# Layer 1's pair loop of a two-layer graph kernel: exponential and lower half moved one pair behind, product three pairs behind

## The reference, cut to what matters

```python
XW = X @ W
Z1 = leaky_relu(s_row[:, None] + s_col[None, :], negative_slope=0.01)   # s_col = XW @ a[:f], s_row = XW @ a[f:]
den = exp(Z1)                                  # 2708 x 2708
num = A @ den
att = where(num != 0, den / num, 0)
H = A @ (att @ XW)
x = layernorm(x + H)
```

## Time and profile before

| | |
|---|---|
| median of 3 runs | 820.3 us (819.61 to 824.0) |
| the profiled execution | 821.94 us, its span 820.2 us |
| layer 1's pair loop, first "ln" to last "ln" | 448.37 to 726.00 us of the span |
| PE, DVE, ACT, POOL busy over the span | 79%, 77%, 52%, 48% |
| mean granted TensorE clock | 0.919 of full |

### The profile page before, as it was taken

The page is one execution under the profiler, slowest core; times in us unless marked ns, Lnnn a source line. Parts: engine busy times, 40 slices in busy tenths (PEclk is TensorE's granted clock), DMA queues, the critical chain, the costliest instruction groups (busy, mean ns, idle before and its releaser), DMA issues.

```text
span 820.2 us, 12721 instructions
## 1 busy us (share of the span) xinstructions
PE 649.0 (79%) x4284; PEld 364.8 (44%) x4284; DVE 634.1 (77%) x1278; ACT 425.0 (52%) x611; POOL 394.1 (48%) x449
## 2 busy tenths in 40 slices
PE   5589999999979898745977678778878778764894
PEld 5244333433329687633532233333333333223783
DVE  3599999999987589988775477787878878782462
ACT  2388888888861156884533254554554555440000
POOL 6378888777770567734717886000000000006685
PEclk9999999999977899955995699999999999995998
DMA  9953444980000000024941000000000000014110
GB/s 210 208 98 68 70 86 84 391 354 1 1 4 1 14 22 14 14 85 136 410 202 46 24 1 1 2 1 1 1 1 2 1 1 2 1 50 134 36 39 24
DMA packets 24554, 58.30 MB, mean 71 GB/s; under 512 B 2634, under 2 KB 13918, under 8 KB 24478
## 3 DMA queue, kind: packets, MB, share of 16 engines
q0 software_dynamic: 7744, 33.39, 16.1%
q1 hardware_dynamic: 16734, 23.92, 8.1%
HBM read 51.59 MB, written 20.96 MB: 88 GB/s over the span
## 4 chain that ended last, share of the span: by engine, by line
DVE 37%; issue 17%; PE 16%; POOL 12%; ACT 12%; DMA 3%; DVEq 2%; POOLq 0%; ACTq 0%; SPq 0%
DVE R L795 7%; DVE ring L786 6%; DVE ring L1198 6%; ACT ring L662 5%; POOL X L439 3%; PE PSALL L1353 3%; DVE ring L1179 2%; PE PSALL L1333 2%; POOL X L462 2%; POOL ring L474 2%; DVE AO L1198 2%; ACT AO L662 2%; PE PSALL L1281 2%; POOL AT L433 2%; DVE R L1108 2%
## 5 line engine op out<-in xcount | busy, mean ns | idle before, releaser
L382 POOL TENSOR_TENSOR R<-R,ring 128x452 f32<-128x452 f32 (+1 forms) x126 | 152.7, 1215 | 33.2 <-ACT ring L503 31.6
L795 DVE SCALAR_TENSOR_TENSOR R<-ring,R 128x452 bf16<-128x452 f32 (+1 forms) x132 | 134.9, 1023 | 0.2
L1541 PE MATMUL PSALL<-AT,R 128*128 x432 | 94.5, 362 | 41.5 <-ACT R L658 39.7
L1333 PE MATMUL PSALL<-R,AO 128*128 128x452 bf16 (+2 forms) x396 | 100.6, 364 | 17.1 <-DVE R L795 16.0
L458 POOL MEMSET R<- 128x108 f32 x1 | 0.2, 188 | 224.0 <-PE PSALL L1577 224.0
L503 ACT ACTIVATE ring<-ring,sm 128x452 f32<-128x452 f32 (+1 forms) x132 | 88.3, 669 | 29.7 <-DVE ring L786 23.5
L1281 PE MATMUL PSALL<-XN 128*128 128x452 f16 (+2 forms) x396 | 98.8, 360 | 4.7 <-issue 4.2
L1353 PE MATMUL PSALL<-R,AT 128*128 128x256 f16 (+1 forms) x792 | 94.1, 279 | 0.0
L1185 DVE TENSOR_TENSOR ring<-ring 128x904 bf16<-128x904 f32 (+1 forms) x50 | 60.6, 1212 | 42.8 <-ACT ring L662 42.8
L511 ACT ACTIVATE R<-ring,sm 128x452 bf16<-128x452 f32 (+1 forms) x132 | 88.6, 671 | 4.3
L662 ACT ACTIVATE ring<-ring 128x904 f32<-128x904 f32 (+1 forms) x50 | 47.8, 956 | 71.3 <-DVE ring L1198 71.3
(11 more groups left out here) (260 smaller groups left out, 1105.2 us busy)
## 6 DMA issues: line engine op xcount, KB each, us to landing
AT<-in_adjT POOLq DMA_DIRECT2D x22, 677.0 KB, 7.1
ATd<-AT SPq DMA_DIRECT2D x2, 7447.0 KB, 31.0
XWd<-ring SPq DMA_DIRECT2D x11, 128.0 KB, 1.8
x1d<-AO SPq DMA_DIRECT2D x1, 1408.0 KB, 6.0
out<-ring SPq DMA_DIRECT2D x21, 64.0 KB, 1.5
Yd<-R SPq DMA_DIRECT2D x1, 768.0 KB, 3.7
Yd<-R SPq DMA_DIRECT2D x1, 640.0 KB, 4.3
AT<-ATd,idx POOLq DMA_INDIRECT x22, 8.5
```

Of the source, the lines that this page charges most:

```text
L382: i = G.tensor_tensor(ES_, ES_, z, ALU.add)
L795: V.scalar_tensor_tensor(F[0:rows, RW:RW + w], z, 1.0, F[0:rows, 0:w], ALU.subtract, ALU.subtract).then_inc(s_low, 1)
L1333: m = TE.matmul(PSALL[:, c, 0:w], half_[0:rows, jt, :], F[0:rows, o:o + w], start=(jt == 0 and k == 0), stop=(jt == T - 1 and k == 2))
L1541: TE.matmul(PSALL[:, b, 0:w], den_h[:, s + q, :, part], AT[:, q:T, c0:c0 + w][:, bass.ds(first, 1), :].rearrange("p o j -> p (o j)"), star ...
```

## The change

`LAG` goes from 2 to 3. On ACT "exp" of pair v-1 follows "ln" of pair v, and "den exp" moves from the turn with cp 0 to that with cp 1, behind that "exp". On DVE "sub" comes first in a pair's turn, then low of v-1, scores of v+1, den scores where cp is 0; "den halves" moves from the turn with cp 1 to the end of the turn with cp 2. A last "exp" follows ACT's loop. No instruction is added, removed or resized.

```diff
-        LAG = 2
+        LAG = 3
@@ scalar
+            def attention_exp(v):
+                av.wait_ge(s_sub, v + 1)
+                S.activation(z_of(v), z_of(v), ACT.Exp).then_inc(s_att1, 1)
+
             for v in range(NV):
...
                 S.activation(tL.rearrange("p (q w) -> p q w", q=2), PSALL[:, 6:8, 0:RW], ACT.Ln, bias=tiny).then_inc(s_ln, 1)
-                if cp == 0 and jt + 1 < T:
+                if v:
+                    attention_exp(v - 1)
+                if cp == 1 and jt + 1 < T:
                     den_exp(jt + 1, 0)
-                av.wait_ge(s_sub, v + 1)
-                S.activation(z_of(v), z_of(v), ACT.Exp).then_inc(s_att1, 1)
                 if cp == 2 and jt + 1 < T:
                     den_exp(jt + 1, 1)
                 if v == 6:
                     S.activation(erb, rb[:, 0:N], ACT.Exp, scale=SLOPE / (1.0 - SLOPE)).then_inc(s_erb, 1)
+            attention_exp(NV - 1)
@@ vector
             for v in range(NV):
                 jt, cp = v // 3, v % 3
+                dv.wait_ge(s_ln, v + 1)
+                dv.wait_ge(s_z1, v + 1)
+                V.tensor_tensor(z_of(v), z_of(v), tL[:, 0:wide_of(v)[1]], ALU.subtract).then_inc(s_sub, 1)
                 if v:
                     attention_low(v - 1)
                 if v + 1 < NV:
                     attention_scores(v + 1)
                 if cp == 0 and jt + 1 < T:
                     den_scores(jt + 1)
-                dv.wait_ge(s_ln, v + 1)
-                dv.wait_ge(s_z1, v + 1)
-                V.tensor_tensor(z_of(v), z_of(v), tL[:, 0:wide_of(v)[1]], ALU.subtract).then_inc(s_sub, 1)
-                if cp == 1 and jt + 1 < T:
+                if cp == 2 and jt + 1 < T:
                     den_halves(jt + 1)
-                if cp == 2 and jt + 1 < T:
                     den_all(jt + 1)
             attention_low(NV - 1)
```

## The result

The changed kernel took 865.9 us (865.3 to 867.3, 4 runs) against 820.2 us (819.6 to 824.0): a ratio of 1.055 (95% interval 1.052 to 1.058), 46 us slower. The forecast was 877, its range 857 to 889. The profiled execution of after took 866.6 us, its span 864.7 us, with a mean granted clock of 0.893 (before 0.919).

What follows compares the result with a forecast made beforehand. Bound by the chain sub, exp, low, scores. Regular tiles +36.5 us, tiles 3, 7, 8, 9 and 19 +17.0, tiles 0 to 2 +2.9, tiles 20 and 21 0: +56 on 821.9, 877 us on the median's basis; range 857 to 889.

Steps and rivals of the forecast that it cites:

- The cycle of the banks: PE with its two banks: 1.30 us from ln to num plus 2.12 us to the next ln, 3.42 us a pair.
- Exp one pair behind: On ACT: exp of the pair before costs nothing and takes 0.96 us off DVE's chain, with 0.1 us to spare.
- The wait on den halves: At each change of tile num starts 4.62 us after ln, not 1.30; a full-clock tile takes 13.58 us against 12.21.
- the opposite case: Rival, kernel gets faster: first num of a tile not held by den halves, under 1.4 us of wait left; chance 0.05.
- The clock: At each change of tile PE idles 3.46 us, its clock falls and the next num takes 1.67 us more.
- the 12 regular tiles: Tiles 4 to 6 and 10 to 18: 15.25 us each against 12.21, together +36.5 us.
- The row that I leaned on: Trace before, behind the long exponential: after a 3.79 us PE gap the clock fell; num took 3.79 us instead of 2.12.
- The upper bound of 2.5 us: Clock loss at a change of tile if the slower clock lasts through the product: 6 matmuls of 2.42 us, not 1.36.
- Product three pairs behind: Scores of v+1 waits for a product ended 2 us earlier: free, except 0.1 us at the end of the loop.
- The start of the loop: Tiles 0 to 2: num of pair 3 ahead of the product, 2.8 us sooner; tiles 1 and 2 slower; together +2.9 us.
- With the clock kept: Rival: the clock stays up through PE's 3.46 us gaps at changes of tile, 33 us less, about 843 us; chance 0.12.
- With den halves in time: Rival: den halves doesn't hold a tile's first num, 10.26 us a tile against 12.21, 787 us; chance 0.05.

Runs made afterwards that it cites:

- The first experiment: The changed kernel with den halves back at the end of the turn with cp 1, one pair earlier: 779.9 us, ratio 0.948.
- the filler kernel: The changed kernel with 12 matmuls more per tile but the first, ahead of num's wait on den halves, results overwritten: 841.7 us, ratio 1.024.
- LAG 2 with early loads: The changed kernel with den halves back at cp 1, LAG 2 again and PE's register loads for the next tile ahead of the product: ratio 0.961.

## Why the prediction was right, and where its size was off

- **The limits.** The cycle of the banks, worked out as 3.42 us, was 3.41 and 3.42 us for a regular "num" at full clock in every kernel in which exp is a pair behind.
- **Exp one pair behind.** Right: low never waits for it, the 0.1 us of room was enough. It is exp alone that moved: low of pair v-1 stood in pair v's turn before the change too, and the lower half that the title has one pair later is den halves. The first experiment shows the gain of exp and the lag together, 42 us.
- **The wait on den halves.** Right in place, count and size: num 4.54 us after ln (forecast 4.62), a tile of 13.5 us at full clock (13.58), and shown as cause by the first experiment and by two more places of the same call. Only the bound for the opposite case was too strict: faster was to need less than 1.4 us of the wait, but with 1.6 us left (2.91 - 1.30, den halves right behind sub) the kernel was already 10 us faster. By the sum's own terms the point is 1.95 us.
- **The clock.** Right in mechanism, mis-sized. The term was 1.67 us at every change of tile. A lost one costs 1.6 to 1.9 us, and 0.4 to 0.5 more where it lasts into the next pair, but only 11 of 18 were lost. Over the 12 regular tiles the forecast was 36.5 us and the measured sum 12 x (14.48 - 12.21) = 27 us: this is nearly the whole difference between the forecast of +57 and the +46 measured. Of these 9 us the clock is 8 (1.67 - 0.98 = 0.69 us a tile, with 14.48 - 13.5 = 0.98 measured), the distances one. The row that I leaned on, one gap of 3.79 us, could not say that a gap of the same length may end either way. Nor was 1.78 us the nearest gap at full clock in that trace: behind the loop PE was idle for 2.46 us up to 766.58 and the granted clock stayed at 1.00, and ahead of the loop a gap of 3.44 us up to 431.43 lost it. The upper bound of 2.5 us comes to 1.67 + 1.06 = 2.73 us by the rows it names; nothing else rests on it. By the Trainium skill's page "TensorE: Matmul & The Clock Gate", section "Loop structure matters more than you think", the loop nest decides whether matmuls stay at speed, and a long wait (for a DMA, in its example) in front of each runs them cold. The filler kernel agrees: with the wait filled, the clock of 520 to 760 us is 1.00 and not 0.91. But 7 of the 18 unfilled waits kept the clock, and there the measurement decides.
- **Product three pairs behind.** "Free" was right for this kernel, as scores comes late in DVE's new turn. It was not for the reason given alone: I looked at the data and the buffers, not at what else is queued behind a wait. In the old order the same LAG costs about 2%, and in the new order LAG 2 costs 0.9 us a tile.
- **The start of the loop.** Its +2.9 us came out as +2.8, in part by luck. The ln of pair 3 was to come 4.62 + 3.35 = 7.97 us after that of pair 2 and came 8.89 us after it, while the two distances before it were 0.95 us shorter than I had left them (9.18 against 10.13). The 3.35 us stand in no row; that num took 3.99 us.
- **The rivals.** With the clock kept I gave 843; the filler kernel took 841.7. With den halves in time I gave 787; the first experiment took 779.9. The second was too high because I had taken little of the gain at the loop's start: the first three tiles took 39.0 us there and 47.8 before.

What stays open: why a gap of one length keeps the clock in one tile and not in the next, why the loop starts later in the second and third group, and what holds the first num of a tile for its last 0.1 us.

## What to carry to other kernels

When a step is moved in an engine's order, follow the smallest instruction that moves with it, and ask which semaphore it alone raises: here 0.59 us of work, moved by one turn, turned a gain of 42 us into a loss of 46. Leave what feeds the next stage where it is early, even if it could be done later. Count an idle gap on TensorE twice: once as a wait and once as the slower matmuls that may follow it. And look for the small register work queued behind a wait before moving a wait: it moves too.

## What the runs showed of the hardware

- Gaps of PE of 3.30 to 3.48 us in the kernel after left the granted clock at full speed 7 times and at half 8 times. Gaps of 2.54 us lost it at 2 of 14 changes of tile with four matmuls put into the gap, and gaps of 2.4 to 2.7 us at 9 of 15 in the old order with den halves at cp 2. Shorter ones lost it now and then: 2.19 us (four matmuls, at 599.12), 1.94 us (LAG 3 alone, at 640.54) and, behind the three-tile window, 1.68 us (LAG 2 with early loads, at 567.62). Those of 1.66 to 1.85 us with den halves right behind sub and those of 1.0 to 1.6 us with twelve matmuls in the gap never did. So the length of the last gap alone does not tell.
- A register load from memory takes 0.30 us on DVE's and on PE's queue (medians of 301, 302, 300 and 296 ns), with 0.15 to 0.19 us of register work behind it. Loads are hidden while the engine has issued work to finish, and exposed once they stand behind a wait that ends late: 0.5 us on DVE, 1.0 us on PE. Put ahead of the waiting instruction they can hold that one up instead: 0.2 us on DVE, 0.6 to 0.7 us on PE.
